# Two-tile scans, four decay banks, shared transpose banks and a strict work order in a fused mixer and feed-forward kernel

## The reference, cut to what matters

```
def step(state, xs):
    d_t, B_t, C_t, u_t = xs
    dA = jnp.exp(d_t[..., None] * A)
    state = dA * state + (d_t * u_t)[..., None] * B_t[:, None, :]
    y_t = jnp.einsum('bdn,bn->bd', state, C_t)
    return (state, y_t)
```

## Time and profile before

| | |
|---|---|
| median of 3 runs | 2127.54 us (2122.42 to 2129.08) |
| profiled execution, span from first to last instruction | 2121.3 us |
| before the first scan | 0 to 126.5 us |
| scan phase | 126.5 to about 2015 us |
| closing rows, after the last scan | about 2015 to 2121 us |
| DVE, POOL, PE and ACT busy in the scan phase | 98%, 92%, 95%, 73% of it |

### The profile page before, as it was taken

The page is one execution under the profiler, slowest core; times in us unless marked ns, Lnnn a source line. Parts: engine busy times, 40 slices in busy tenths (PEclk is TensorE's granted clock), DMA queues, the critical chain, the costliest instruction groups (busy, mean ns, idle before and its releaser), DMA issues.

```text
span 2121.3 us, 30643 instructions
## 1 busy us (share of the span) xinstructions
PE 2016.8 (95%) x10530; PEld 1523.7 (72%) x10530; DVE 1956.7 (92%) x2374; ACT 1479.3 (70%) x2193; POOL 1813.5 (85%) x778
## 2 busy tenths in 40 slices
PE   8999999999999799999999997999999999899998
PEld 6877778886565577788776555878875557686686
DVE  4459999999999999999999999999999999999944
ACT  5488787887576776777976657677796656957632
POOL 4369998879998999888899998988799998899950
PEclk9999999999999999999999999999999999999999
DMA  8777866653333357655563333585464437444441
GB/s 310 266 262 264 285 193 223 207 176 118 92 121 92 125 167 261 228 189 169 185 187 110 110 99 103 172 282 176 143 204 111 113 93 242 152 165 133 130 145 40
DMA packets 168666, 362.95 MB, mean 171 GB/s; under 512 B 18688, under 2 KB 45440, under 8 KB 168512
## 3 DMA queue, kind: packets, MB, share of 16 engines
q1 hardware_dynamic: 167312, 360.31, 52.8%
q10 hardware_dynamic: 1200, 0.69, 0.1%
HBM read 292.08 MB, written 68.85 MB: 170 GB/s over the span
## 4 chain that ended last, share of the span: by engine, by line
DVE 34%; PE 33%; issue 12%; POOL 6%; ACT 6%; DMA 1%; SPq 1%; DVEq 0%; POOLq 0%; ACTq 0%
DVE drive L1437 19%; PE bank L1306 9%; DVE y_acc L1462 8%; PE state_t L1251 8%; POOL drive L1915 4%; PE bank L1283 3%; PE bank L1285 3%; PE bank L1284 3%; DVE channels L1469 3%; ACT decay L1695 1%; DVE channels L1506 1%; PE bank L1251 1%; DVE rows L1516 1%; POOL y_acc L1920 1%; DMA w_split<-w_split 1%
## 5 line engine op out<-in xcount | busy, mean ns | idle before, releaser
L1915 POOL TENSOR_TENSOR drive<-delta_u,b_bcast 128x2048 f32<-128x2048 f32 x255 | 1168.4, 4584 | 71.9 <-PE state_t L1251 64.7
L1437 DVE TENSOR_TENSOR_SCAN drive<-decay,drive 128x512 f32<-128x512 f32 x1024 | 1192.6, 1203 | 7.4 <-ACT decay L1695 4.0
L1695 ACT ACTIVATE decay<-delta,a_sb 128x512 f32<-128x512 f32 x1024 | 693.8, 688 | 348.0 <-DVE drive L1437 343.1
L1251 PEld LDWEIGHTS state_t<-identity,drive 128*128 128x128 f32 x4096 | 479.4, 142 | 252.9 <-DVE drive L1437 76.5
L1251 PE MATMUL state_t<-identity,drive 128*128 128x128 f32 x4096 | 575.3, 277 | 52.5 <-DVE drive L1437 31.0
L1283 PE MATMUL bank<-cols_high,w_split 128*128 128x512 f32 (+1 forms) x1248 | 526.7, 422 | 25.6 <-DVE cols_low L1581 9.6
L1462 DVE SCALAR_TENSOR_TENSOR y_acc<-state_t,c_rows,y_acc 128x512 f32<-128x512 f32 x699 | 494.2, 731 | 13.4 <-PE state_t L1251 11.6
L1285 PE MATMUL bank<-cols_high,w_split 128*128 128x512 f32 (+1 forms) x1248 | 491.9, 394 | 0.0
L1284 PE MATMUL bank<-cols_low,w_split 128*128 128x512 f32 (+1 forms) x1248 | 489.1, 392 | 0.0
L1306 PE MATMUL bank<-channels,w_raw 128*128 128x512 f32 x896 | 422.8, 593 | 2.0 <-ACT delta L1806 1.5
L1920 POOL TENSOR_TENSOR y_acc<-y_acc,scaled 128x512 f32<-128x512 f32 x261 | 336.1, 1288 | 77.7 <-ACT scaled L1715 77.3
(11 more groups left out here) (217 smaller groups left out, 1421.2 us busy)
## 6 DMA issues: line engine op xcount, KB each, us to landing
w_split<-w_split SPq DMA_DIRECT2D x304, 512.0 KB, 4.2
b_bcast<-b_rows SPq DMA_DIRECT2D x255, 256.0 KB, 3.5
w_raw<-in_w_out SPq DMA_DIRECT2D x112, 256.0 KB, 3.0
w_raw<-in_w_in SPq DMA_DIRECT2D x64, 256.0 KB, 4.4
gates<-scratch SPq DMA_DIRECT2D x64, 256.0 KB, 3.7
scratch<-gates SPq DMA_DIRECT2D x64, 256.0 KB, 4.6
out<-rows SPq DMA_DIRECT2D x16, 512.0 KB, 4.2
w_raw<-in_x_cols SPq DMA_DIRECT2D x24, 256.0 KB, 4.2
```

The source lines that it names most:

```text
L1251: last = engine.transpose(bank[0:tile.shape[1], i * P:(i + 1) * P], tile, identity[:, :])
L1437: engine.tensor_tensor_scan(state, decay[(GT * s + t) % DECAYS][:, :], state, 0.0, ALU.mult, ALU.add).then_inc(signal["scan"])
L1695: engine.activation(decay[i % DECAYS][:, :], delta[:, g % 2, t, :], ACT.Exp, scale=a_sb[:, j, n:n + 1]).then_inc(signal["decay"])
L1915: engine.tensor_tensor(drive[key % DRIVES][:, :, :], du[:, :, :], row, ALU.mult).then_inc(signal["drive"])
```

## The change

**Scans over two tiles.** The four decay tiles of a unit are now one PSUM tensor `decays` of four banks. One scan covers tiles 0 and 1, one covers 2 and 3, each 128x1024: 512 scans. So that the second tile doesn't inherit the first one's last state, column 0 of each decay bank is set to zero once at the start (one small memset), and ACT writes columns 1 to 511 only. A scan now waits for both its decays, and a decay for the pair scan that last read its bank.

**Shared banks.** The two `state_t` banks go. There are four general banks, and each turn takes one of them, in turn with the products, the other transposes, the first sequence's `ssm_mm` and `b_spread`.

**Strict order.** The shift tables and the two layings-out are replaced by a table `ORDER`: one rank per piece of work, over all engines. Each engine takes its pieces in rank order, and of each pool of buffers too the takers are served in rank order. `None` marks the one of `add` and `scale` + `sum` that isn't done. The table makes 680 adds (699 before) and 280 scale + sum (261 before).

```
-BANKS, SCRATCH, RAW, SPLIT = 3, 4, 4, 4
+BANKS, SCRATCH, RAW, SPLIT = 4, 4, 4, 4
-DECAYS, TURNED, DRIVES = 3, 2, 3
+DECAYS, DRIVES = 4, 3
+SCANS = ((0, 1), (2, 3))
+def scan_of(s, t):
+    return "scan", (s, t // 2)
+ORDER = {
+    "x_load": [2, 3, 5, 14, 13, 7, 18, 8],
...
     def put(self, engine, due, us, stage, key, needs=(), take=(), give=(), spare=0, kb=0):
-        if self.known is None:
-            due += shift_of(stage, key)
...
+        i = self.nth[stage] = self.nth.get(stage, -1) + 1
+        if stage in ORDER:
+            if ORDER[stage][i] is None:
+                return
+            due = ORDER[stage][i]
...
+                    name = queues[e][0]
+                    if left[name] > 0 or any(takers[pool][0] != name or len(free[pool]) < ...
                         continue
...
-            put("DVE", i, 1.13, "scan", (s, t), [drive_of(s, t), ("decay", (s, t))],
+            put("DVE", i, 2.2, "scan", (s, pair), [*dict.fromkeys(drive_of(s, t) for t in tiles), *[("decay", (s, t)) for t in tiles]],
...
-        state_banks = [psum(f"state_t{i}", [P, GT * P]) for i in range(TURNED)]
-        decay = [psum(f"decay{i}", [P, T]) for i in range(DECAYS)]
+        decays = psum("decays", [P, DECAYS, T])
+        decay = [decays[:, i, :] for i in range(DECAYS)]
...
-                    turned(state_banks[i % TURNED], [states[:, t, tt * P:(tt + 1) * P] for t in range(GT)]).then_inc(signal["turn"])
+                    turned(bank_of("turn", key), [states[:, t, tt * P:(tt + 1) * P] for t in range(GT)]).then_inc(signal["turn"])
...
+            engine.memset(decays[:, :, 0:1], 0.0).then_inc(starts_zeroed)
...
-                    engine.tensor_tensor_scan(state, decay[(GT * s + t) % DECAYS][:, :], state, 0.0, ALU.mult, ALU.add).then_inc(signal["scan"])
+                    state = drive[s % DRIVES][:, tiles, :].rearrange("p a t -> p (a t)")
+                    engine.tensor_tensor_scan(state, decays[:, tiles, :].rearrange("p a t -> p (a t)"), state, 0.0, ALU.mult, ALU.add).then_inc(signal["scan"])
...
-                        e.wait_ge(*done("scan", divmod(i - DECAYS, GT)))
-                    engine.activation(decay[i % DECAYS][:, :], delta[:, g % 2, t, :], ACT.Exp, scale=a_sb[:, j, n:n + 1]).then_inc(signal["decay"])
+                        e.wait_ge(*done(*scan_of(*divmod(i - DECAYS, GT))))
+                    e.wait_ge(starts_zeroed, 1)
+                    engine.activation(decay[i % DECAYS][:, 1:T], delta[:, g % 2, t, 1:T], ACT.Exp, scale=a_sb[:, j, n:n + 1]).then_inc(signal["decay"])
```

More of the change, by code:

```diff
@@ L445, in arrange @@
         free = {pool: [(i, None, None) for i in range(size)] for pool, size in self.pools.items()}
-        ready = {e: [] for e in ENGINES}
         at = {e: 0.0 for e in ENGINES}
-        now, dma, ends, finished, wanted, table, dropped = 0.0, 0.0, [], 0, len(self.pieces), None, set()
-        for name, piece in self.pieces.items():
-            if left[name] == 0:
-                ready[piece["engine"]].append((piece["due"], piece["order"], name))
-        while finished < wanted:
-            for e in ENGINES:
-                for entry in sorted(ready[e]) if at[e] <= now else []:
-                    piece = self.pieces[entry[2]]
-                    if at[e] > now or any(len(free[pool]) < piece["spare"] + sum(x == pool for x, _ in piece["take"]) or
-                                          pool in queues and queues[pool][0] != entry[:2] for pool, _ in piece["take"]):
+        now, dma, ends, finished, table = 0.0, 0.0, [], 0, None
@@ L458, in arrange @@
+        while finished < len(self.pieces):
+            begun = True
+            while begun:
+                begun = False
+                for e in ENGINES:
+                    if at[e] > now or not queues[e]:
                         continue
-                    on = piece["ahead_of"]
-                    if on and (at[on] > now + FREE_IN or any(due < entry[0] - DUE_EARLIER for due, _, _ in ready[on])):
+                    name = queues[e][0]
+                    piece, used = self.pieces[name], {pool for pool, _ in self.pieces[name]["take"]}
+                    if left[name] > 0 or any(takers[pool][0] != name or len(free[pool]) < piece["spare"] + sum(x == pool for x, _ in piece["take"])
+                                             for pool in used):
@@ L485, in arrange @@
                         end = dma + self.DELAY[e]
-                    ends += [(at[e], piece["order"], entry[2], True), (end, piece["order"], entry[2], False)]
+                    ends += [(at[e], piece["order"], name, True), (end, piece["order"], name, False)]
             ends.sort()
-            coming = [ends[0][0]] if ends else []
-            coming += [at[e] for e in ENGINES if at[e] > now and ready[e]]
-            assert coming, ("nothing can go on", now, {e: sorted(r)[:4] for e, r in ready.items()},
-                            {p: len(f) for p, f in free.items()})
-            now = min(coming)
+            assert ends, ("nothing can go on", now, {e: q[:2] for e, q in queues.items()}, {p: len(f) for p, f in free.items()})
+            now = ends[0][0]
             while ends and ends[0][0] <= now:
@@ L659, in y_job @@
         put("PE", due - TURN_FIRST, 0.45, "y_turn", key, [summed(last, tt) for tt in range(TT)],
-            take=[("bank", ("y_turn", key))],
-            give=[("bank", ("state", i)) for i in range(TURNED)] if last == len(UNITS) - 1 and t == 0 else [])
+            take=[("bank", ("y_turn", key))])
         put("DVE", due + 0.3, 0.655, "y_skip", key, [("y_turn", key), du_of(b, g, 1)], give=[("bank", ("y_turn", key))])
@@ L1457, in _ @@
                     b, g, n = UNITS[s]
[L1458 removed]
+                    c, bank = c_rows[b % 2][:, tt, n:n + 1], banks[place["bank", ("turn", key)]]
                     e.wait_ge(*done("turn", key))
@@ L1698, in _ @@
                     b, g, n = UNITS[s]
-                    bank = state_banks[(TT * s + tt) % TURNED]
+                    bank = banks[place["bank", ("turn", key)]]
                     e.wait_ge(*done("turn", key))
@@ L1709, in _ @@
                     b, g, n = UNITS[s]
-                    bank, prior = state_banks[(TT * s + tt) % TURNED], before["scaled", key]
+                    bank, prior = banks[place["bank", ("turn", key)]], before["scaled", key]
                     e.wait_ge(*done("turn", key))
```

535 lines of the change are left out of this document (221 added, 314 removed), and 340 rows, old and new, of tables (EARLIER, JOB_SHIFTS, ORDER).

## The result

| | before | after |
|---|---|---|
| median of 4 runs each, same chip | 2126.93 us (2122.42 to 2129.08) | 2104.08 us (2102.61 to 2105.88) |
| ratio, 95% interval | | 0.9896 (0.9882 to 0.9910) |
| profiled execution, span | 2121.3 us | 2104.0 us |
| scan phase (first to last scan) | 126.5 to 2015.7, 1889.2 us | 130.1 to 1999.0, 1868.9 us |

The forecast was 2101 us, 26 us less than before; it became 22.9 us less by the medians. The two profiled spans differ by only 17.3 us. After's profiled execution took 2105.88 us, 1.9 more than its span, and was its slowest; in a run of before 2125.6 us also stood beside a span of 2123.7, so before's profiled execution took about 2123.2 and was among its fastest. The traces are read for where time went, the medians for how much.

What follows compares the result with a forecast made beforehand. DVE was taken to bound the scan phase, PE and POOL close behind. Merge 26 plus adds 12 gave 38 us, less 6 for saturated stretches and 6 for decay waits: 26 off 2127.5, 2101 us; forecast 2085 to 2115, wider range 2068 to 2131.

Steps and rivals of the forecast that it cites:

- VectorE's list: Scan phase: merging and moved adds cut DVE's busy time by 26 + 12 = 38 us, from 1854 to 1816.
- The spacing of a pair: Scans on DVE: a pair takes 2.18 instead of 2.24 us, so 512 merges save 0.05 each, 26 us.
- The whole fixed part of 0.14 us: Rival, scans on DVE: each merge saves its record's full 0.14 us; 72 us gain, 2056 us; chance 0.03.
- stretches that PE and POOL fill: Saturated 300 of the scan phase's 1888 us: a DVE gain there is worth nothing, 6 us taken off.
- late decays: Scans waiting for ACT: a pair waits for its later decay, waits grow from 4.0 to about 10, costing 6 us.
- An add finds its turn done: DVE's adds: the new order puts more scans ahead of them, so turns are ready; no separate size given.
- Adds moved off: 19 fewer adds on DVE at 0.65 us: 12 us less there, 13 us more on ACT, 24 on POOL.
- Shared banks: PE's turns: costed at nothing; PE's waits for adds and scales to free a bank should fall below 89 us.
- Unchanged within 2 us: Sign: the phases before 126 us and after the last scan stay the same within 2 us.
- The later decay: Rival, ACT's 77 table returns: pairs need two decays, 0.62 us more each, 48 us; 2138 us; chance 0.12 with other order harm.
- Gaps closed: Rival, scan phase: the order halves DVE's idle 34 us and full stretches ease; 55 us gain, 2072 us; chance 0.15.
- PE and POOL take it back: Rival, scan phase: their full stretches spread and DVE waits longer; gain only 8 us, about 2119 us; chance 0.20.

Runs made afterwards that it cites:

- split: Changed kernel with its order, banks and waits, but each pair scanned by two 128x512 instructions; 2120.72 us, ratio 0.9974 to the kernel before.
- adds_back: Changed kernel with 19 of the adds it had moved to ACT and POOL put back on VectorE; 2114.82 us, ratio 0.9939 to the kernel before.
- pairs: Kernel before with pair scans and a fourth decay bank, turned states cut to one bank, order replanned; 2688.68 us, ratio 1.2631.
- pad_dve: Changed kernel with 256 more VectorE memsets of 128x24, one behind a scan in each unit; 2108.90 us, ratio 0.9916 to the kernel before.

## Why the prediction was right

*VectorE's list.* Forecast -38 us, measured -34.3. The spacing of a pair was met to the second digit (2.18), and a merge saved 0.043 us of busy time instead of 0.05. The whole fixed part of 0.14 us wasn't there to be saved; the overlap of about 0.09 us between a record and the next start had taken most of it already. The rule of the Trainium skill's page "VectorE: DVE Perf Modes", section on the TRN2 errata, would make the saving 157 ns, an estimate from that page; the 0.043 us measured don't bear it out for these scans.

*What comes through.* The forecast took off 6 us for stretches that PE and POOL fill and 6 us for late decays, so that 26 of 38 (0.68) were left. Measured it was 20.3 of 34.3 (0.59) over the phase, 17.3 (0.50) over the profiled span and 22 (0.64) by the timed runs, and in the single steps, over their phases, 14.8 of 22.2 (0.67) for the merge and 10.9 of 13.1 (0.83) for the adds. The fraction was near, its reasons mostly were not, so that the total came out some 3 us off is in part luck. Decays were no later than before, 4.4 us; of the full stretches only the early one kept the merge's gain back. The loss stands before the adds, 9 us more of waits for turns. "An add finds its turn done", which the forecast read from the order, was wrong: those waits rose from 11.6 to 15.6 us with the order, the banks and the moved adds, and to 20.8 with the merge. PE's list just ahead of such a late turn shows how: before, a product stood there in 13 of 15 cases in the scan phase (8.5 us); in the changed kernel that is 26 of 42 (some 13 us). In six further cases (3.6 us; seven in split, none before) PE itself had waited for an add or a scale to free a bank. That VectorE's shorter list, against a PE list of the same length, is what makes it arrive early more often is the likely reading and wasn't tested by itself.

*Adds moved off.* 12 us off VectorE's list forecast, 13.1 measured, and worth 9 us of time (5 to 13). The rival in which POOL takes them back is out for these 19, and for the 19 after them the time did come back, though more through ACT's and PE's lateness than through POOL's drives.

*Shared banks.* PE's waits for adds and scales fell as forecast: the loader's from 74 to 50 us, PE's own for adds only from 14.9 to 14.1, 65 in all against 89. But these figures leave out what else now waits for the same banks. Over all of PE's work it was 94 us before, 99 in split, which has the shared banks and the order, 94 in adds_back and 79 in the changed kernel. The fall came with VectorE's shorter list, not with the banks. Whether the sharing alone is worth or costs any time wasn't isolated; the kernel pairs shows that the turns can't give the merge its bank by going down to one.

*Head and tail.* "Unchanged within 2 us" failed for the first scan (+3.6) and held for what matters: the second drive began at 137.0 against 137.2, and the tail was 0.6 us shorter.

*The other rivals.* The later decay would have shown as scans waiting about 48 us for ACT; it was 4.4. Gaps closed would have shown as less idle time on VectorE; it rose by 14, to 48, above the 35 to 45 that the forecast named. Of "PE and POOL take it back" a part is true: the idle time that came is mostly waits for PE, but 22 us of gain are left and not 8. What of the gain is due to the order by itself wasn't isolated; the order of the kernel before wasn't tried with pairs and shared banks. By subtraction (22 less 17 less 9) the order, the shared banks and the other swapped blocks together are worth -4 us, good to 5, which can't be told from nothing.

## What to carry to other kernels

Here the busiest engine had 2% of idle time and two others were at 92%, and a cut in its list was worth half to four fifths of itself, two thirds for the merge. So work a cut out by spacing from start to start, and then take a part off; and don't expect the next cut to do the same, since nineteen more adds moved off made this kernel 15 us slower. A merge of two instructions saved what spacing showed beside the streaming columns, not the fixed part of a record. When a sign of the forecast comes true, look whether a run without the supposed cause shows it too: PE's shorter waits for banks were put down to their sharing and came with VectorE's shorter list. Before mending a wait at the head, look for who waits for the next step.

## What the runs showed of the hardware

Two operations of VectorE with both inputs in SBUF slowed down beside work of POOL that reads SBUF. The two `delta_u` products of the head, and POOL at that time, first of the kernel before, then of the changed one:

```profile
123.90 1.29 DVE L1443 TENSOR_TENSOR delta_u<-delta,channels 128x512 f32<-128x512 f32 x2 [4.07 <-ACT delta L1806]
```

```profile
121.38 2.55 POOL L1940 TENSOR_TENSOR w_split<-w_raw,w_split 128x512 fp32r<-128x512 f32 x2 [2.06 <-ACT w_split L1736]
127.12 1.29 POOL L1940 TENSOR_TENSOR w_split<-w_raw,w_split 128x512 fp32r<-128x512 f32 x1 [3.19 <-ACT w_split L1736]
```

```profile
123.15 2.75 DVE L1640 TENSOR_TENSOR delta_u<-delta,channels 128x512 f32<-128x512 f32 x2 [3.49 <-ACT delta L2004]
```

```profile
121.12 4.23 POOL L2138 TENSOR_TENSOR w_split<-w_raw,w_split 128x512 fp32r<-128x512 f32 x3 [3.81 <-ACT w_split L1934]
```

With POOL idle but for the first 0.04 us the two took 1.29 us, beside it 2.75, 1.5 us more; POOL's three took 4.23 us, 0.4 more than three of its 1.28. The single records look like taking turns: VectorE's two last 1.06 and 1.77 us, and each ends 0.55 us after one of POOL's does. It cost no time here, since the step behind them waited 2.9 us more for PE. This is one place in one trace. The scans, which read one input from a bank of PSUM, show nothing like it, though POOL is busy 94% of their phase (duration ns least, median, most):

```profile
L1634 DVE TENSOR_TENSOR_SCAN drive<-decays,drive x512: 2236/2277/2293, 130.1 to 1996.7; 128x1024 f32<-128x1024 f32 x171
```

And the small memsets cost less of VectorE than their records say. These, of pad_dve, have records of 78 ns, 20.0 us in all, and added 7 us to VectorE's busy time, 0.03 us apiece, since they overlap their neighbours' records:

```profile
L1637 DVE MEMSET no_use_rows<- 128x24 f32 x256 | 20.0, 78 | 0.0
```
